# Issuing the softmax-denominator broadcast one key tile later, and per-chunk waits in the last transposes

## The reference

```
x = layernorm(x + outer_attention(x))
x = layernorm(x + ffn_net(x))
```

```
h = shift_token(x)
q, k, v = split(h @ wqkv)                 # 8 heads of 64
q, k = l2norm(q) * qs, l2norm(k) * ks     # then rotary embedding with scales
o = local_attention(q, k, v)              # windows of 512: own and previous window, causal, scores times 8
x = x + o @ wo
h = layernorm(shift_token(x)) @ w1 + b1   # 1024 -> 2 * 2730
x = x + (a * gelu(g)) @ w2 + b2           # a, g are the halves of h
```

## Time and profile before

| What | us |
|---|---|
| median of the 2 runs | 8539.83 |
| the 2 runs | 8340.17, 8739.49 |
| the profiled execution | 8385.2 |
| span of its slowest core (core 0) | 8383.4 |
| spans of its eight cores | 8319.0 to 8383.4 |

### The profile page before, as it was taken

The page is one execution under the profiler, slowest core; times in us unless marked ns, Lnnn a source line. Parts: engine busy times, 40 slices in busy tenths (PEclk is TensorE's granted clock), DMA queues, the critical chain, the costliest instruction groups (busy, mean ns, idle before and its releaser), DMA issues. The chain is left out here.

```text
span 8383.4 us, 72806 instructions; the slowest of 8 cores (8319.0 to 8383.4 us)
## 1 busy us (share of the span) xinstructions
PE 5726.2 (68%) x21696; PEld 2057.5 (25%) x21696; DVE 2309.7 (28%) x4472; ACT 2492.5 (30%) x4771; POOL 635.4 (8%) x944
## 2 busy tenths in 40 slices
PE   1129776777777647777749779777777749779853
PEld 0014121221222212222214324322222214333321
DVE  1101222220110144333421321323433421321347
ACT  0002556667667512222211111102232221111101
POOL 0010000000000010000001111100000011111100
PEclk5559688888889866666659889886666669889876
DMA  9992001110100142113146656732212056756643
GB/s 78 82 89 84 6 16 31 31 31 1 31 22 4 26 86 67 36 35 71 25 90 79 96 98 79 96 92 51 56 36 71 26 95 80 96 100 89 80 141 141
DMA packets 694033, 531.90 MB, mean 63 GB/s; under 512 B 426620, under 2 KB 560092, under 8 KB 693664
## 3 DMA queue, kind: packets, MB, share of 16 engines
q0 software_dynamic: 472720, 208.37, 24.4%
q1 hardware_dynamic: 220944, 318.86, 15.5%
HBM read 466.56 MB, written 176.19 MB: 77 GB/s over the span
## 5 line engine op out<-in xcount | busy, mean ns | idle before, releaser
L1361 PE MATMUL p_pb<-p_hn,p_w 128*128 128x512 bf16 (+1 forms) x5632 | 1247.3, 385 | 223.9 <-DVE p_hn L1277 149.1
L600 ACT ACTIVATE p_pt<-p_pss 128x512 bf16<-128x512 f32 (+3 forms) x2304 | 1168.6, 559 | 484.6 <-PE p_pss L368 291.5
L383 PE MATMUL p_psz<-p_pt,p_v 128*65 128x512 bf16 x2304 | 782.2, 425 | 183.1 <-DVE p_zt L496 103.2
L1361 PEld LDWEIGHTS p_pb<-p_hn,p_w 128*128 128x128 bf16 (+1 forms) x5632 | 556.1, 99 | 916.8 <-issue 273.1
L368 PE MATMUL p_pss<-p_qtb,p_kt 64*128 64x512 bf16 (+3 forms) x2304 | 558.7, 406 | 229.9 <-ACT p_pt L600 218.1
L1376 PE MATMUL p_pb<-p_h,p_w 128*128 128x512 bf16 (+1 forms) x2816 | 650.8, 386 | 31.0 <-DVE p_x L1300 22.9
L1107 ACT ACTIVATE p_pt<-p_pb 128x128 bf16<-128x128 f32 (+1 forms) x960 | 367.7, 435 | 748.6 <-PE p_pb L889 747.5
L896 PE MATMUL p_pb<-p_pt,p_vr 128*65 128x512 bf16 x960 | 501.8, 630 | 107.2 <-DVE p_pt L1023 104.2
L1328 ACT ACTIVATE p_glu<-p_pb,p_bc 128x512 bf16<-128x512 f32 x352 | 242.0, 687 | 1094.3 <-PE p_pb L1361 1094.2
L1287 DVE SCALAR_TENSOR_TENSOR p_h<-p_pb,p_bc,p_glu 128x512 bf16<-128x512 f32 x352 | 264.3, 751 | 962.6 <-PE p_pb L1361 962.6
L828 PE MATMUL p_pb<-p_xq,p_wqkv 128*128 128x512 bf16 x1024 | 263.6, 425 | 325.4 <-PEq L772 198.4
(11 more groups left out here) (158 smaller groups left out, 5324.1 us busy)
## 6 DMA issues: line engine op xcount, KB each, us to landing
p_w<-w POOLq DMA_DIRECT2D x336, 256.0 KB, 4.9
p_xf<-xf SPq DMA_DIRECT2D x16, 2048.0 KB, 13.5
xf<-p_x POOLq DMA_DIRECT2D x128, 256.0 KB, 6.2
xb<-p_x POOLq DMA_DIRECT2D x256, 128.0 KB, 5.1
p_hf<-xf SPq DMA_DIRECT2D x32, 1024.0 KB, 8.6
p_xr<-xf SPq DMA_DIRECT2D x16, 2048.0 KB, 9.7
xf<-p_x SPq DMA_DIRECT2D x128, 256.0 KB, 3.0
xf<-p_stage SPq DMA_DIRECT2D x32, 512.0 KB, 30.6
```

The costliest lines, as they stand in the source:

```text
L383: t.matmul(ps_z[ZBANK[h]][0:65, 0:512], v_bf[:, kt * 520 + g * 65:kt * 520 + g * 65 + 65], pt[GS % 8][:, 0:512], start=(kt == 0), stop=(kt ...
L600: s.activation(pt[GS % 8][:, off:512], ps_s[GS % 3][:, off:512], AF.Exp, scale=0.125).then_inc(sE.sem, 1)
L1361: inst = t.matmul(pb[bank + gi % 2][0:jw, :] if jw < 128 else pb[bank + gi % 2][:, :], w1buf[:, (seq % 4) * NC * 128 + kc * jw: (seq % 4) ...
```

## The change

In both attentions the broadcast of the previous pair's reciprocals is issued behind the scores of key tile 1 of the new pair, where it was issued behind those of key tile 0. In the last stage each transpose of a block's first token tile waits for its own normalized chunk, where the first of them waited for all eight.

```diff
@@ _p1_outer_attn, TensorE
                         emit_S(hA, kt)
                         emit_S(hB, kt)
-                        if p >= 1 and kt == 0:
+                        if p >= 1 and kt == 1:
                             emit_pair_bcast(p - 1)
                         if kt >= 1:
                             t.wait_ge(sE.sem, b_sE + sidx[(hB, kt - 1)])
@@ _p2_inner_attn, TensorE
                         emit_S(h0, ki)
                         emit_S(h1, ki)
-                        if hp >= 1 and ki == 0:
+                        if hp >= 1 and ki == 1:
                             emit_pair_bcast(hp - 1)
                         if ki >= 1:
                             t.wait_ge(sE.sem, sE0 + sidx[(h1, ki - 1)])
@@ _p6_final, TensorE
                         if g >= 4:
                             t.wait_ge(vev.sem, b_vev + g - 3)
-                        if ttile == 0 and c == 0:
-                            t.wait_ge(vxn.sem, b_vxn + (qb + 1) * NC)
+                        if ttile == 0:
+                            t.wait_ge(vxn.sem, b_vxn + qb * NC + c + 1)
                         t.transpose(ps_t[g % 4][:, 0:128],
```

## The result

The changed kernel is slower than the one before: the ratio of their times is 1.0159, with a 95% interval of 1.0099 to 1.0219, so whether it is slower by more than 2% is not decided. Forecast was 8514 on 8385.2, which is 1.0154. The ratio therefore rests on two runs of the changed kernel, 8480.74 and 8517.33 us, and six of the one before.

The account below looks back on a forecast made before the run. No engine is full; chains of waits at head-pair borders bound the kernel, and a later broadcast delays all behind it. 51 + 13 + 59 + 11 - 5.6 = +129 us on 8385.2 gives 8514, range 8440 to 8670.

Parts of the forecast that it names:

- the term for the mixed median: Whole kernel: two earlier runs' median lies 155 us above the profiled execution, so a mixed median would be near 8669.
- 1.05 us a border: Outer attention, blocks 1 to 7: the broadcast, and all behind it, comes 1.05 us later at 49 borders, 51 us.
- forecast 13: Outer attention, block 0: diagonal scores delay the broadcast by 1.81 us at each of 7 borders, 13 us.
- forecast 1.90: Inner attention, block 0: the broadcast comes 1.90 us later at each of 6 borders, 11 us.
- forecast 1.41: Inner attention, blocks 1 to 7, two layers: the broadcast comes 1.41 us later at 42 borders, 59 us.
- forecast 5.6: Last stage, 8 blocks: VectorE's 0.70 us wait before its first copy goes, 5.6 us gained.
- My sum for the outer stage: Outer attention: 51 us for blocks 1 to 7 plus 13 us for block 0, with no extra slow-clock steps.
- rival 1: Outer borders: longer TensorE idling adds four lower-clock steps at 49 borders, 57 us more, 8571 in total; chance 0.14.
- my two signs of being wrong: Scores of key tile 1 start before the denominators end, or the outer blocks' granted clock falls by more than 0.02.
- Rival 2: Not slower: earlier exps cover the later broadcast if exps release PV(0), gaining 8 and 5.6 us, 8371; chance 0.05.
- Rival 3: All borders: overlap and later waits swallow part of the delay, leaving about +73 us, 8458; chance 0.11.

Follow-up runs that it names:

- e9: Kernel before plus matmuls nobody reads (6 per outer border, 4 per inner) where TensorE waits for the denominators; outer attention 2038 to 2051 us, against 2051 to 2054.
- e10: Changed kernel plus the same unread filler matmuls at the borders of both attentions; outer attention 2097 to 2101 us, against 2125 to 2127 without them.
- e7: Changed kernel with PV two key tiles behind the scores instead of one, broadcast in the new position; 1.0043 of the time of the kernel before.
- e5: Changed kernel with the next pair's first scores ahead of the last PV, their exps ahead of the denominators, broadcast in its old position; outer 2100 to 2106 us.
- e6: Changed kernel with the next pair's first scores ahead of the last PV, their exps ahead of the denominators, broadcast in the new position; outer 2097 to 2100 us.

## Why the prediction was right or wrong

**The range failed; the mechanism held.** The recorded median of 8883.78 lies outside 8440 to 8670. The step that failed is the term for the mixed median: "their median 8539.83 lies 155 above the profiled execution", which set the upper end in "How the numbers follow", "8670 (the mixed median)". I had two runs of the kernel before, 400 us apart, took their middle, and did not ask what the median is if most runs are like the longer one. Ten of the changed kernel's twelve were, so the median lies among them: 370 us above the forecast of 8514, where the term had 155. From the longer run alone it would have been 8739.49 + 129 = 8868; the ten lie between 8733.20 and 8962.65, so that this is close is in part luck. The two others, 8480.74 and 8517.33, are inside the range. Why ten of twelve were like that stays open, and the change is not shown to be the cause: the kernel before had 4 of 10 such runs here, and 6 of 7, 5 of 17 and 6 of 12 in the three later groups.

The forecast of +129 us against 132 in the stages is right in its mechanism, and in part lucky in its size: the outer attention costs 9 us more than I had, the inner one 7 less, and the last stage gains 1 to 2 less.

**The outer attention, blocks 1 to 7.** I had 1.05 us a border; from exp(A0) to exp(2) the borders show 1.06. S(1) starts at 0.75 us after exp(A0) (0.74 forecast), and the time from a broadcast to PV(0), which I took as fixed, is 3.10 us in the old position and 3.11 in the new. What follows exp(2) is another matter: see "The clock".

**Block 0 and the inner attention.** Outer block 0 grew by 12 us, forecast 13. A border of a block with four key tiles costs (47.8 - 42.5) / 3 = 1.8 us in the inner attention, forecast 1.90. A border of the others costs (87.2 - 83.5) / 3 = 1.23 us, forecast 1.41. The mis-sized term is S(1): I had let the broadcast start 0.22 us behind the last mask. In the trace it starts 0.08 behind it (mask 3309.31, broadcast 3309.39). Summed over 48 borders this stage costs 63 us where I had 70.

**The last stage.** 4 to 5 us gained, forecast 5.6; the wait of 0.21 us for the fifth transpose is what I left out.

**The clock.** My sum for the outer stage was 64 us, the trace has 73. The granted clock over blocks 0 to 7 (without the first pairs), before and after:

```profile
900.00:2880.00 1980.00, 1427.96 (x5482) 402.29 (x5481) 339.87 (x710) 1321.12 (x2540) 21.36 (x40) 0.87 0.07 18
```

```profile
912.00:2960.00 2048.00, 1449.41 (x5485) 406.51 (x5484) 342.96 (x718) 1321.92 (x2542) 21.31 (x40) 0.85 0.07 18
```

It fell from 0.87 to 0.85, but that is a mean over unlike blocks. Nearly all of the fall is block 1, whose clock was 0.75 to 0.81 before and is 0.54 to 0.61 now, and that block costs 22 us where I had 7.4: 15 us more, about a quarter of rival 1's 57. Blocks 2 to 7 cost 39 us where I had 44. So rival 1 came true in one block and in no other, which the sum had as nothing, and one of my two signs of being wrong ("if the granted clock of the outer blocks falls by more than 0.02") was seen there. e9 and e10 support that the clock is the reason: at one and the same granted clock of the stage, 0.90, the move costs 53 us and not 73, and block 1, whose clock there does not fall, costs 3 us and not 22. It is not fully separated, because at the higher clock S(1) is shorter too, and why block 1 loses its clock and block 2 does not was not tested. The Trainium skill's rule (that activity releases the lower clock, section on the HAM clock gate of "TensorE: Matmul & The Clock Gate") agrees in its direction with 0.90 in the kernels with fillers.

**The other rivals.** Rival 2 (not slower) is out: its condition, slack between VectorE's end and what else PV(0) needs, did not hold at any border read, and e7 shows that even a tile of look-ahead does not make it. Rival 3 (half of it vanishes) is out: 132 us against 129 forecast.

**What I said would be seen.** The wait left L393 for L368; L383 waits 2.5 us each (141.7 / 57), as forecast; ScalarE's idle before exp(2) is 3.57 (3.5 forecast). Wrong was that the 42 waits of L896 would grow by as little as the outer ones: they grew from 2.5 to 3.6 us each. A long outer block should have become 7.4 us longer; block 1 became 22 longer and the others 4 to 9.

## What to carry to other kernels

A wait that an instruction reorder removes from one place is gone only if the instruction that moves ahead is itself free to run; look up what it waits for, and in which queue that stands. Here S(1) was bound to an exp behind the denominators on ScalarE, so moving it ahead of the broadcast only delayed the one thing that the rest of the chain needed. When three engines pass a result round at a border, as here, let the engine that idles look one tile further ahead (PV two tiles behind the scores, -1.4%), and keep the broadcast at the earliest place at which its input is ready. And read the granted clock block by block: a fall of 0.02 in the mean of a stage was a fall of 0.2 in one block of eight.

## What the runs showed that I had not expected

The cost of an edit can be nothing or 73 us depending on an order on another engine (e5 and e6 against before and after). About 1 us more of waiting at each border kept all pairs of one block (block 1, core 0) at TensorE's lower level, and cost it some 15 us on top of the waiting, while its neighbours kept their clock. And fillers that keep TensorE busy through one wait do little if a second of 2 us or more follows (outer stage 2052 to 2046), but 30 us when that second wait is down to 0.5 us (1993 to 1962).
